# A two-layer recurrent kernel: the same instructions in another order on three engines

## Chip, cores and metric

The kernel runs on one core of one Trainium2 chip. The metric is device time in microseconds (us) of one execution, taken as the median of several executions. A smaller number is better.

## What is computed

The input `x` is 64 sequences (B) of 64 steps (S) of 256 features (D), all float32. Two layers are added to it one after the other.

```python
# layer 0: gated, written with cumulative sums (no step-by-step dependence in the matmuls)
f = sigmoid(x @ W_f.T + b_f); i = sigmoid(x @ W_i.T + b_i)
r = f / (f + i + EPS);        q = i / (f + i + EPS)
cand = x @ W_h.T + b_h
L = cumsum(log(r + EPS), axis=1)                  # over the 64 steps
scaling_t = exp(L_last - L_(t-1))                 # product of (r + EPS) from t to the end
hidden = cumsum(scaling * q * cand, axis=1) + exp(L) * cond
x1 = x + hidden
# layer 1: a plain recurrence of 64 dependent steps
h_t = tanh(x1_t @ Wx + b + h_(t-1) @ Wh),   h_0 = cond
out = x1 + h
```

## The kernel before

Features lie on the 128 partitions (two halves of 128), and the columns are steps times batch. The 64 steps are cut into eight chunks of eight steps, so a whole chunk of a tensor is 128 partitions by 1024 columns, and one step is 128 by 128. Each engine has its own instruction list, written out by hand as a list of calls; engines run their lists strictly in that order and meet through semaphores. There is no scheduler: what a list holds is what runs, and an instruction that waits holds up all that stand behind it on its engine.

**Layer 0, the gates.** The chunks are handled backwards, n = 0 being chunk 7, because the suffix product runs from the last step to the first.

- TensorE: `transpose_x(n)` turns a chunk of `x` (8 transposes, into one fixed pair of PSUM banks, free again when `chunk_split(n-1)` is done and filled from rows that a DMA has landed). `transpose_w(g)` turns weight g. `gates(n, g)` makes 12 matmuls of 512 columns for gate g (products of a high and a low part, so it needs `x_hi`, `wt_hi`, `wt_lo` and, for its last third, `x_lo`). `candidate(m)` does the same for the candidate, in the chunk order 7, 6, 5, 0, 3, 4, 1, 2. `transpose_cond` turns the initial state.
- ScalarE: `split_x(n)` and `split_w(g)` copy the rounded high part out of PSUM; `layer1_weight` does so for `Wx`. `sigmoids(n)` is four activations of 512 columns. `inverses((n, ...))` loads another table of functions, takes Ln and Exp of the denominators (1/den), and the next `sigmoids` loads the first table again. `move_candidate(c)` copies a candidate from PSUM to SBUF.
- VectorE: `chunk_split(n)` and `weight_split(g)` take the low part by subtraction. `denominator(n)` adds the gates; `ratio(n)` and `i_by_den(n)` multiply by the inverse. `suffix(n, t)`, 128 columns, multiplies the suffix product by one more step, t from 7 down to 0; each needs the one before it. `by_suffix` multiplies q by the suffix products, `product`, `product_first` and `moved_product` by the candidate.

**Between the layers.** `chain(c, s, e)` runs the cumulative sum and the cumulative product over steps s to e (instructions of 128 columns in two interleaved chains), `plus_decay` and `first_layer` add up `x1` in the tile `den`; chunks 0 and 1 do so in halves of four steps. For chunks 2 to 7 ScalarE's `split_x1` and VectorE's `x1_rest` split `x1` into high and low parts for TensorE.

**Layer 1.** TensorE adds `h @ Wh` to the projections `x1 @ Wx` in PSUM, ScalarE does the tanh, 64 steps one after the other. Projections of the next chunk and transposes of the output are put into the slots between the recurrence's matmuls, two slots to a step. The first steps use only the first half of chunk 0; TensorE waits for the second half of it in slot 6 and for all of chunk 1 in slot 9:

```python
for bank in SECOND_HALF.get(slot, ()):
    pe.wait_ge(x1_ready, 2)
    project_native(0, bank, second_half)
```

While VectorE finishes layer 0, TensorE runs matmuls whose results nobody reads (`keep_warm`), each released by a semaphore of VectorE's.

The line numbers of the profile that matter: L263 `split_x`, L267 `split_w`, L278 `sigmoids`, L286 and L289 `inverses`, L299 `layer1_weight`, L316 `split_x1`, L395 `chunk_split`, L400 `weight_split`, L409 `denominator`, L415 `ratio`, L419 `i_by_den`, L445 `suffix`, L541 and L537 `first_layer`, L546 `x1_rest`, L503 and L511 `chain`, L770 and L781 transposes, L790 to L796 gates and candidates, L903 and L911 projections, L932 the recurrence.

Of the kernel before, what the change touches and what calls it, by code (L numbers as in the profile page):

```python
# [26 lines left out]
def build(nc, x, cond, w_f, b_f, w_i, b_i, w_h, b_h, wx, wh, b_x, out):  # L27
# [10 lines left out]
    with ExitStack() as ctx:  # L38
# [107 lines left out]
        def chunk_of(n):  # L146
            return NCH - 1 - n
# [105 lines left out]
        def _(act):  # L253
# [7 lines left out]
            def split_x(n):  # L261
                act.wait_ge(xt_in_psum, n + 1)
                nc.scalar.activation(x_hi[:, chunk_of(n)], ps[:, XT:XT + 2], ACT.Copy).then_inc(x_hi_ready, 1)  # L263

            def split_w(g):
                act.wait_ge(wt_in_psum, g + 1)
                nc.scalar.activation(wt_hi[:, g], ps[:, WT[g]].rearrange("p (a h) -> p a h", a=HALVES), ACT.Copy)\  # L267
                    .then_inc(wt_hi_ready, 1)
# [28 lines left out]
            def layer1_weight():  # L297
                act.wait_ge(wx_landed, 16)
                nc.scalar.activation(wx_hi[:, :, :], wx_f[:, :, :], ACT.Copy).then_inc(wt_hi_ready, 1)  # L299
# [28 lines left out]
            def move_candidate(c):  # L328

                m = CAND_ORDER.index(c)  # L330
                if MOVED_TO[c] == "den 3":
                    act.wait_ge(i_inv_ready, NCH)
                    act.wait_ge(u_ready, NCH)
                if MOVED_TO[c] == "den 2":
                    act.wait_ge(i_inv_ready, NCH - 1)
                    act.wait_ge(u_ready, NCH - 1)
                if MOVED_TO[c] == "rows 0":
                    act.wait_ge(xt_in_psum, NCH - 1)
                if MOVED_TO[c] == "rows 1":
                    act.wait_ge(xt_in_psum, NCH)  # L340
                for a in range(HALVES):
                    act.wait_ge(cand_in_psum, 2 * m + a + 1)
                    nc.scalar.activation(MOVED[c][:, a], ps[:, CAND_BANK[m] + a], ACT.Identity,
                                         bias=bias[:, 2, a:a + 1]).then_inc(cand_moved, 1)

            split_x(0)
            split_w(0)
            split_w(1)
            split_w(2)
            split_x(1)  # L350
            sigmoids(0)
            split_x(2)
            inverses((0,))
            sigmoids(1)
            split_x(3)
            layer1_weight()
            first_state()
            sigmoids(2)
            split_x(4)
# [11 lines left out]
            inverses((7,))  # L371
            move_candidate(4)
            move_candidate(1)
            nc.scalar.preload_act_table_set("sigmoid_and_others")
            move_candidate(2)
            for c in range(NCH):
                for t in range(T):
                    tanh(c, t)
# [12 lines left out]
        def _(dve):  # L391
# [6 lines left out]
            def weight_split(g):  # L398
                dve.wait_ge(wt_hi_ready, g + 1)
                nc.vector.tensor_tensor(wt_lo[:, g], ps[:, WT[g]].rearrange("p (a h) -> p a h", a=HALVES),  # L400
                                        wt_hi[:, g].bitcast(F32), ALU.subtract).then_inc(wt_lo_ready, 1)
# [10 lines left out]
            def ratio(n):  # L412
                c = chunk_of(n)
                dve.wait_ge(inv_ready, n + 1)
                nc.vector.tensor_tensor(r_d[:, c + 1], r_d[:, c + 1], den[:, n % RING], ALU.mult).then_inc(u_ready, 1)  # L415

            def i_by_den(n):
                dve.wait_ge(inv_ready, n + 1)
                nc.vector.tensor_tensor(q_s[:, chunk_of(n)], q_s[:, chunk_of(n)], den[:, n % RING], ALU.mult)\  # L419
                    .then_inc(i_inv_ready, 1)  # L420
# [167 lines left out]
            chunk_split(1)  # L588
            denominator(0)
            chunk_split(2)  # L590
            i_by_den(0)
            ratio(0)
            weight_split(2)
            chunk_split(3)
            denominator(1)
            suffix(0, 7)
            suffix(0, 6)
            suffix(0, 5)
            suffix(0, 4)
            suffix(0, 3)  # L600
            denominator(2)
            chunk_split(4)
            suffix(0, 2)
            suffix(0, 1)
            suffix(0, 0)
            by_suffix(0)
            product(7)
            ratio(1)
            ratio(2)
            suffix(1, 7)  # L610
            suffix(1, 6)
            suffix(1, 5)
            suffix(1, 4)
            i_by_den(1)
            suffix(1, 3)
            suffix(1, 2)
            layer1_weight_rest()
            suffix(1, 1)
            chunk_split(5)
            suffix(1, 0)  # L620
            suffix(2, 7)
            suffix(2, 6)
            by_suffix(1)
            suffix(2, 5)
            suffix(2, 4)
            suffix(2, 3)
            suffix(2, 2)
            suffix(2, 1)
            denominator(3)
            denominator(4)  # L630
            chunk_split(6)
            i_by_den(2)
            suffix(2, 0)
            ratio(3)
            i_by_den(3)
            suffix(3, 7)
            suffix(3, 6)
            i_by_den(4)
            suffix(3, 5)
            suffix(3, 4)  # L640
            suffix(3, 3)
            chunk_split(7)
            suffix(3, 2)
            denominator(5)
            suffix(3, 1)
            ratio(4)
            suffix(3, 0)
            suffix(4, 7)
            by_suffix(2)
            suffix(4, 6)  # L650
            suffix(4, 5)
            denominator(6)
            suffix(4, 4)
            suffix(4, 3)
            suffix(4, 2)
            suffix(4, 1)
            product(6)
            suffix(4, 0)
            i_by_den(5)
            ratio(5)  # L660
            ratio(6)
            suffix(5, 7)
            denominator(7)
            suffix(5, 6)
            product(5)
            suffix(5, 5)
            suffix(5, 4)
            suffix(5, 3)
            suffix(5, 2)
            suffix(5, 1)  # L670
            suffix(5, 0)
            suffix(6, 7)
            suffix(6, 6)
            suffix(6, 5)
            suffix(6, 4)
            i_by_den(6)
            suffix(6, 3)
            suffix(6, 2)
            suffix(6, 1)
            ratio(7)  # L680
            suffix(6, 0)
            suffix(7, 7)
            suffix(7, 6)
            suffix(7, 5)
            suffix(7, 4)
            i_by_den(7)
            suffix(7, 3)
            suffix(7, 2)
            suffix(7, 1)
            suffix(7, 0)  # L690
            by_suffix_first(0)
            product_first(0)
            chain(0, 0, 4)
            plus_decay(0, 0)
            by_suffix_first(1)
            by_suffix(6)
            first_layer(0, 0)
            product_first(1)
            moved_product(1)
            chain(0, 4, 8)  # L700
            chain(1, 0, 4)
            plus_decay(0, 1)
            plus_decay(1, 0)
            first_layer(0, 1)
            chain(1, 4, 8)
            product(3)
            plus_decay(1, 1)
            first_layer(1, 0)
            first_layer(1, 1)
            by_suffix(5)  # L710
# [2 lines left out]
            chain(2, 4, 8)  # L713
            plus_decay(2, None)
            first_layer(2, None)
            by_suffix(4)
            by_suffix(3)
            x1_rest(2, 0)
            x1_rest(2, 1)
            moved_product(4)  # L720
            chain(3, 0, 4)
            chain(3, 4, 8)
            plus_decay(3, None)
            first_layer(3, None)
            x1_rest(3, 0)
            x1_rest(3, 1)
            chain(4, 0, 4)
            chain(4, 4, 8)
            plus_decay(4, None)
            first_layer(4, None)  # L730
            x1_rest(4, 0)
            chain(5, 0, 4)
            x1_rest(4, 1)
            chain(5, 4, 8)
            plus_decay(5, None)
            chain(6, 0, 4)
            chain(6, 4, 8)
            first_layer(5, None)
            chain(7, 0, 4)
            chain(7, 4, 8)  # L740
            x1_rest(5, 0)
            x1_rest(5, 1)
            plus_decay(6, None)
            first_layer(6, None)
            plus_decay(7, None)
            first_layer(7, None)
            x1_rest(6, 0)
            x1_rest(6, 1)
            x1_rest(7, 0)
            x1_rest(7, 1)  # L750
            out_sum_first()
# [10 lines left out]
        def _(pe):  # L762
# [98 lines left out]
            transpose_x(0)  # L861
            transpose_w(0)
            transpose_w(1)
            gates(0, 0)
            transpose_x(1)
            transpose_w(2)
            transpose_cond()
            gates(0, 1)
            transpose_x(2)
            gates(1, 0)  # L870
            gates(1, 1)
            transpose_x(3)
# [1 line left out]
            gates(2, 1)  # L874
            transpose_x(4)
            candidate(0)
            transpose_x(5)
            gates(3, 0)
            gates(3, 1)
            gates(4, 0)  # L880
            gates(4, 1)
# [4 lines left out]
            transpose_x(7)  # L886
            gates(6, 0)
            gates(6, 1)
            gates(7, 0)
            gates(7, 1)  # L890
            candidate(2)
            candidate(3)
            candidate(4)
            candidate(5)
# [160 lines left out]
```

## Time and profile before

| what | value |
|---|---|
| median of 3 executions | 194.7 us (194.15 to 194.71) |
| profiled execution, its own time | 194.83 us |
| its span in the trace | 193.0 us |
| busy over the span: TensorE, VectorE, ScalarE | 180.9, 131.7, 115.4 us |
| mean granted TensorE clock | 0.987 of full |

The span runs from the first instruction to the last; 1.8 us of the execution's time lie outside it. Busy time is a sum over stages that have different limits: VectorE does most of its work in the first 130 us, TensorE's busy time includes the matmuls that only keep it going.

### The profile page before, as it was taken

How to read it: one execution, taken by the hardware profiler on the slowest of the kernel's cores; microseconds unless marked ns; L12 is line 12 of the kernel's file. 1: busy time of each engine (PE TensorE's matmuls, PEld its weight loads, DVE VectorE, ACT ScalarE, POOL GpSimd, SP SyncE). 2: the span in 40 equal slices, each digit the busy share in tenths (PEclk: the TensorE clock that was granted, in tenths of full speed). 3: DMA queues.
4: the chain of work that ended last, by engine and by line, in shares of the span. 5: the costliest groups of instructions: out<-in, count | busy, mean ns of one | idle time of the engine just before them, and what ended most of it. 6: DMA issues, size and time to landing. Idle time of an engine off the chain costs nothing.

```text
span 193.0 us, 3133 instructions
## 1 busy us (share of the span) xinstructions
PE 180.9 (94%) x1178; PEld 161.4 (84%) x1178; DVE 131.7 (68%) x292; ACT 115.4 (60%) x235; POOL 24.4 (13%) x28
## 2 busy tenths in 40 slices
PE   6799999999999995999989999999999999999990
PEld 6678878888888884787879989999999999999880
DVE  0044569999998999999999999795999520200121
ACT  3309998996996897162223264656556565645550
POOL 1000000200100011131011210222211222221000
PEclk9999999999999998899999999999999999999998
DMA  5994340750320019299003035625374473627326
GB/s 112 246 250 115 109 109 19 171 138 3 59 51 0 0 33 184 41 190 192 15 5 54 5 49 93 128 41 131 51 153 69 77 141 56 135 38 154 59 48 169
DMA packets 12910, 17.83 MB, mean 92 GB/s; under 512 B 2080, under 2 KB 10720, under 8 KB 12896
## 3 DMA queue, kind: packets, MB, share of 16 engines
q0 software_dynamic: 4960, 7.87, 24.8%
q1 hardware_dynamic: 6848, 9.77, 19.5%
q10 hardware_dynamic: 1088, 0.00, 0.3%
q8 instruction: 9, 0.15, 0.3%
q14 instruction: 5, 0.04, 0.1%
HBM read 5.57 MB, written 4.19 MB: 51 GB/s over the span
## 4 chain that ended last, share of the span: by engine, by line
PE 53%; DVE 23%; ACT 14%; issue 5%; DMA 2%; SPq 0%; DVEq 0%
PE ps L932 29%; PE ps L903 9%; DVE suf L445 6%; DVE den L409 3%; PE ps L941 3%; PE ps L911 3%; ACT den L289 3%; DMA x_rows<-in_x 2%; PE ps L790 2%; ACT L278 2%; PE ps L796 2%; DVE q_s L430 2%; PE ps L792 2%; PE ps L781 2%; DVE q_s L419 2%
## 5 line engine op out<-in xcount | busy, mean ns | idle before, releaser
L932 PE MATMUL ps<-h_t,wh_f 128*128 128x128 f32 x504 | 69.3, 278 | 1.0 <-ACT h_t L309 0.7
L309 ACT ACTIVATE h_t<-ps,bias 128x64 f32<-128x64 f32 x128 | 37.2, 314 | 49.1 <-PE ps L932 43.7
L932 PEld LDWEIGHTS ps<-h_t,wh_f 128*128 128x128 f32 x504 | 62.2, 191 | 4.4 <-ACT h_t L309 3.3
L790 PE MATMUL ps<-x_hi,wt_lo 128*128 128x512 f32 x96 | 38.8, 404 | 3.1 <-DVE q_s L457 2.1
L792 PE MATMUL ps<-x_hi,wt_hi 128*128 128x512 f32 x96 | 38.2, 398 | 0.0
L796 PE MATMUL ps<-x_lo,wt_hi 128*128 128x512 f32 x96 | 30.3, 398 | 0.0
L243 POOL DMA_DIRECT2D den<-h_t x14 | 16.7, 1191 | 73.4 <-ACT h_t L309 73.4
L790 PEld LDWEIGHTS ps<-x_hi,wt_lo 128*128 128x128 f32 x96 | 18.3, 191 | 7.6 <-issue 3.9
L796 PEld LDWEIGHTS ps<-x_lo,wt_hi 128*128 128x128 f32 x96 | 18.5, 194 | 4.3 <-DVE x_lo L395 0.3
L792 PEld LDWEIGHTS ps<-x_hi,wt_hi 128*128 128x128 f32 x96 | 18.3, 191 | 3.6
L445 DVE SCALAR_TENSOR_TENSOR suf<-r_d,suf 128x128 f32<-128x128 f32 x64 | 18.5, 290 | 1.8
L546 DVE TENSOR_TENSOR x_lo<-den,x_hi 128x512 fp32r<-128x512 f32 x12 | 8.0, 692 | 16.6 <-ACT x_hi L316 16.6
L511 DVE SCALAR_TENSOR_TENSOR r_d<-r_d 128x128 f32<-128x128 f32 x64 | 18.6, 290 | 0.1
L503 DVE TENSOR_TENSOR q_s<-q_s 128x128 f32<-128x128 f32 x63 | 18.3, 291 | 0.0
L235 POOL DMA_DIRECT2D x_lo<-x_hi x8 | 7.0, 877 | 80.2 <-PE ps L796 80.2
L903 PE MATMUL ps<-x_hi,wx_lo 128*128 128x256 f32 x48 | 14.6, 319 | 0.0
L395 DVE TENSOR_TENSOR x_lo<-ps,x_hi 128x1024 fp32r<-128x1024 f32 x8 | 9.8, 1222 | 6.6 <-ACT x_hi L263 6.6
L903 PE MATMUL ps<-x_hi,wx_hi 128*128 128x256 f32 x48 | 13.6, 296 | 0.0
L278 ACT ACTIVATE q_s<-ps,bias 128x512 f32<-128x512 f32 x16 | 10.6, 692 | 3.4 <-PE ps L796 3.4
L263 ACT ACTIVATE x_hi<-ps 128x1024 fp32r<-128x1024 f32 x8 | 8.3, 1032 | 6.0 <-PE ps L781 6.0
L419 DVE TENSOR_TENSOR q_s<-q_s,den 128x1024 f32<-128x1024 f32 x8 | 9.8, 1220 | 2.2 <-ACT den L289 2.2
L409 DVE SCALAR_TENSOR_TENSOR den<-r_d,q_s 128x1024 f32<-128x1024 f32 x8 | 9.7, 1221 | 1.7 <-ACT q_s L278 1.6
(62 smaller groups left out, 232.3 us busy)
## 6 DMA issues: line engine op xcount, KB each, us to landing
x_rows<-in_x SPq DMA_DIRECT2D x16, 256.0 KB, 4.2
x_lo<-x_hi POOLq DMA_DIRECT2D x8, 512.0 KB, 5.2
den<-h_t POOLq DMA_DIRECT2D x14, 256.0 KB, 3.8
out_x<-x_rows SPq DMA_DIRECT2D x14, 256.0 KB, 3.2
out_x<-x_rows SPq DMA_DIRECT2D x2, 192.0 KB, 2.7
h_t<-in_L_cond_W_f SPq DMA_DIRECT2D x1, 256.0 KB, 4.8
h_t<-in_L_cond_W_i SPq DMA_DIRECT2D x1, 256.0 KB, 6.1
h_t<-in_L_cond_W_h SPq DMA_DIRECT2D x1, 256.0 KB, 7.4
```

Of the source, the lines that this page charges most:

```text
L243: nc.gpsimd.dma_start(den[:, c % RING, :, half_cols(th)], h_t[:, c % 2, :, half_cols(th)], accum_op=ALU.add).then_inc(o_sum[c % 2][th], 16)
L278: nc.scalar.activation(to, ps[:, 2 * g + a], ACT.Sigmoid, bias=bias[:, g, a:a + 1])\
L309: nc.scalar.activation(h_t[:, c % 2, a, cols(t)], ps[:, 4 * (c % 2) + 2 * a + t % 2, cols(t // 2)], ACT.Tanh, bias=bias[:, 3, a:a + 1])\
L409: nc.vector.scalar_tensor_tensor(den[:, n % RING], r_d[:, c + 1], EPS, q_s[:, c], ALU.add, ALU.add)\
L445: nc.vector.scalar_tensor_tensor(suf[:, n % SUF, :, cols(t)], r_d[:, c + 1, :, cols(t)], EPS, after, ALU.add, ALU.mult).then_inc(suf_steps, 1)
L503: nc.vector.tensor_tensor(now, now, before, ALU.add).then_inc(s_steps, 1)
L511: nc.vector.scalar_tensor_tensor(now, now, EPS, before, ALU.add, ALU.mult).then_inc(d_steps, 1)
L790: last = nc.tensor.matmul(to, w_lo[:, dk, rows], x_hi[:, c, dk], start=dk == 0, stop=False, skip_group_check=True)
L792: last = nc.tensor.matmul(to, w_hi[:, dk, rows], x_hi[:, c, dk], start=False, stop=False, skip_group_check=True)
L796: last = nc.tensor.matmul(to, w_hi[:, dk, rows], x_lo[:, c, dk], start=False, stop=dk == 1, skip_group_check=True)
L903: nc.tensor.matmul(ps[:, 4 * (c % 2) + bank, steps.start * B:steps.stop * B], w[:, part, a * P:(a + 1) * P], moving, start=first, stop=Fal ...
L932: return nc.tensor.matmul(bank[:, :, cols(t // 2)], wh_f[:, dk, a * P:(a + 1) * P], twice, start=False, stop=dk == 1, skip_group_check=True)
```

## The change

No instruction is added or taken out. Three lists are put into another order; every call keeps its waits and its semaphores.

```diff
@@ ScalarE @@
+            split_w(0)
             split_x(0)
-            split_w(0)
+            split_x(1)
             split_w(1)
             split_w(2)
-            split_x(1)
+            layer1_weight()
             sigmoids(0)
...
             split_x(3)
-            layer1_weight()
             first_state()
...
             move_candidate(1)
+            move_candidate(2)
             nc.scalar.preload_act_table_set("sigmoid_and_others")
-            move_candidate(2)
@@ VectorE, from denominator(0) to the suffix products of n = 1 @@
             denominator(0)
             chunk_split(2)
-            i_by_den(0)
             ratio(0)
+            suffix(0, 7)
             weight_split(2)
-            chunk_split(3)
-            denominator(1)
-            suffix(0, 7)
             suffix(0, 6)
             suffix(0, 5)
             suffix(0, 4)
             suffix(0, 3)
-            denominator(2)
-            chunk_split(4)
             suffix(0, 2)
             suffix(0, 1)
             suffix(0, 0)
+            chunk_split(3)
+            denominator(1)
+            i_by_den(0)
+            denominator(2)
+            layer1_weight_rest()
+            chunk_split(4)
             by_suffix(0)
             product(7)
...
```

From here to n = 7 the `denominator`, `i_by_den`, `ratio`, `chunk_split` and `product` calls are put between other `suffix` calls than before (one at a time rather than in groups of two to four; `product(6)` and `product(5)` come earlier). After the last suffix product:

```diff
             by_suffix_first(0)
             product_first(0)
+            by_suffix_first(1)
+            by_suffix(6)
             chain(0, 0, 4)
             plus_decay(0, 0)
-            by_suffix_first(1)
-            by_suffix(6)
+            product_first(1)
             first_layer(0, 0)
-            product_first(1)
             moved_product(1)
             chain(0, 4, 8)
+            plus_decay(0, 1)
             chain(1, 0, 4)
-            plus_decay(0, 1)
-            plus_decay(1, 0)
             first_layer(0, 1)
             chain(1, 4, 8)
+            plus_decay(1, 0)
+            plus_decay(1, 1)
             product(3)
-            plus_decay(1, 1)
             first_layer(1, 0)
             first_layer(1, 1)
...
             first_layer(2, None)
+            x1_rest(2, 0)
             by_suffix(4)
-            by_suffix(3)
-            x1_rest(2, 0)
             x1_rest(2, 1)
-            moved_product(4)
             chain(3, 0, 4)
             chain(3, 4, 8)
             plus_decay(3, None)
             first_layer(3, None)
+            by_suffix(3)
+            moved_product(4)
             x1_rest(3, 0)
             x1_rest(3, 1)
...
             first_layer(4, None)
+            chain(5, 0, 4)
+            chain(5, 4, 8)
             x1_rest(4, 0)
-            chain(5, 0, 4)
+            chain(6, 0, 4)
             x1_rest(4, 1)
-            chain(5, 4, 8)
@@ TensorE @@
             transpose_w(0)
             transpose_w(1)
+            transpose_x(1)
             gates(0, 0)
-            transpose_x(1)
             transpose_w(2)
-            transpose_cond()
             gates(0, 1)
             transpose_x(2)
+            transpose_cond()
             gates(1, 0)
...
             candidate(0)
+            gates(3, 0)
             transpose_x(5)
-            gates(3, 0)
             gates(3, 1)
...
             gates(6, 1)
+            candidate(2)
             gates(7, 0)
             gates(7, 1)
-            candidate(2)
             candidate(3)
```

## Rows read from the trace of the kernel before

**Rows 1.** Stretches of the span: length, busy time of each engine, granted clock, DMA.

```profile
28.00:99.00 71.00, 67.87 (x329) 56.20 (x327) 67.71 (x137) 49.74 (x65) 7.02 (x8) 0.98 0.38 76
99.00:188.00 89.00, 88.01 (x726) 84.40 (x726) 53.55 (x143) 48.53 (x149) 16.67 (x14) 1.00 0.44 80
```

**Rows 2.** Waits: who waited for whom, us in total, times, longest.

```profile
DVE x_lo L395 <- ACT x_hi L263: 6.6, 3, 4.5
DVE q_s L419 <- ACT den L289: 2.2, 1, 2.2
DVE den L409 <- ACT q_s L278: 1.6, 2, 1.2
...
PE ps L911 <- DVE den L541: 0.7, 1, 0.7
```

**Rows 3.** VectorE's timeline: start, us, instruction, idle before it and releaser.

```profile
9.23 0.69 DVE L400 TENSOR_TENSOR wt_lo<-ps,wt_hi 128x512 fp32r<-128x512 f32 x1 [8.20 <-ACT wt_hi L267]
...
27.84 1.23 DVE L395 TENSOR_TENSOR x_lo<-ps,x_hi 128x1024 fp32r<-128x1024 f32 x1 [1.68 <-ACT x_hi L263]
...
75.22 3.32 DVE L445 SCALAR_TENSOR_TENSOR suf<-r_d,suf 128x128 f32<-128x128 f32 x10
...
91.26 0.69 DVE L541 TENSOR_TENSOR den<-den,q_s 128x512 f32<-128x512 f32 x1
...
102.34 1.30 DVE L541 TENSOR_TENSOR den<-den,q_s 128x512 f32<-128x512 f32 x2
```

**Rows 4.** Chain of work that ended last, 96 to 100 us: start, us, what.

```profile
96.09 0.20 DVE q_s L503
...
98.96 0.71 PE ps L911 x4
```

**Rows 5.** ScalarE's timeline in the first 32 us.

```profile
7.69 1.02 ACT L263 ACTIVATE x_hi<-ps 128x1024 fp32r<-128x1024 f32 x1 [5.46 <-PE ps L781]
...
9.45 0.60 ACT L267 ACTIVATE wt_hi<-ps 128x512 fp32r<-128x512 f32 x1 [0.24 <-PE ps L770]
...
17.11 1.37 ACT L278 ACTIVATE q_s<-ps,bias 128x512 f32<-128x512 f32 x2
...
22.09 1.06 ACT L289 ACTIVATE den<-den 128x1024 f32<-128x1024 f32 x1
...
31.02 0.69 ACT L278 ACTIVATE q_s<-ps,bias 128x512 f32<-128x512 f32 x1 [0.67 <-PE ps L796]
```

**Rows 6.** TensorE's timeline in the first 18 us.

```profile
7.49 0.60 PE L770 MATMUL ps<-ident,h_t 128*128 128x128 f32 x4
8.75 0.66 PE L770 MATMUL ps<-ident,h_t 128*128 128x128 f32 x4 [0.66 <-DMA h_t<-in_L_cond_W_i]
...
14.73 0.50 PE L790 MATMUL ps<-x_hi,wt_lo 128*128 128x512 f32 x1
...
17.13 0.62 PE L796 MATMUL ps<-x_lo,wt_hi 128*128 128x512 f32 x2
17.59 1.03 PE L781 MATMUL ps<-ident,x_rows 128*128 128x128 f32 x8
```

**Rows 7.** The DMAs of the second chunk of x, issued at 3.14 and 3.66 us.

```profile
DMA to landing us min/median/max: 6.5/6.9/7.4
```

**Rows 8.** TensorE's timeline after its longest pause before the recurrence.

```profile
74.79 0.47 PE L790 MATMUL ps<-x_hi,wt_lo 128*128 128x512 f32 x1 [2.10 <-DVE q_s L457]
```

**Rows 9.** The stretch behind that pause (columns as Rows 1).

```profile
75.60:79.00 3.40, 3.40 (x10) 2.66 (x9) 3.03 (x10) 0.38 (x1) 0.00 (x0) 0.51 0.42 77
```

**Rows 10.** ScalarE's timeline in the recurrence: splits of x1.

```profile
112.93 1.14 ACT L316 ACTIVATE x_hi<-den 128x512 fp32r<-128x512 f32 x2
...
131.28 0.62 ACT L316 ACTIVATE x_hi<-den 128x512 fp32r<-128x512 f32 x1
```

**Rows 11.** TensorE's timeline in the recurrence: first readers of the low parts.

```profile
116.32 0.40 PE L903 MATMUL ps<-x_lo,wx_hi 128*128 128x256 f32 x2
...
125.55 0.28 PE L903 MATMUL ps<-x_lo,wx_hi 128*128 128x256 f32 x1
```

More of the change, by code:

```diff
@@ L610, in _ @@
             suffix(1, 7)
+            i_by_den(1)
             suffix(1, 6)
@@ L613, in _ @@
             suffix(1, 4)
-            i_by_den(1)
             suffix(1, 3)
             suffix(1, 2)
-            layer1_weight_rest()
             suffix(1, 1)
+            suffix(1, 0)
             chunk_split(5)
-            suffix(1, 0)
+            denominator(3)
             suffix(2, 7)
+            by_suffix(1)
             suffix(2, 6)
-            by_suffix(1)
+            i_by_den(2)
             suffix(2, 5)
+            denominator(4)
             suffix(2, 4)
             suffix(2, 3)
+            product(6)
             suffix(2, 2)
+            chunk_split(6)
             suffix(2, 1)
[L629 to L632, printed above, removed]
+            ratio(3)
             suffix(2, 0)
-            ratio(3)
+            suffix(3, 7)
+            by_suffix(2)
+            suffix(3, 6)
             i_by_den(3)
-            suffix(3, 7)
-            suffix(3, 6)
-            i_by_den(4)
             suffix(3, 5)
             suffix(3, 4)
+            i_by_den(4)
             suffix(3, 3)
-            chunk_split(7)
             suffix(3, 2)
-            denominator(5)
             suffix(3, 1)
@@ L648, in _ @@
             suffix(4, 7)
-            by_suffix(2)
+            chunk_split(7)
             suffix(4, 6)
+            denominator(5)
             suffix(4, 5)
@@ L655, in _ @@
             suffix(4, 2)
+            product(5)
             suffix(4, 1)
-            product(6)
+            ratio(5)
             suffix(4, 0)
+            suffix(5, 7)
+            suffix(5, 6)
             i_by_den(5)
[L660 to L665, printed above, removed]
             suffix(5, 5)
@@ L669, in _ @@
             suffix(5, 2)
+            ratio(6)
             suffix(5, 1)
@@ L672, in _ @@
             suffix(6, 7)
+            denominator(7)
             suffix(6, 6)
@@ L675, in _ @@
             suffix(6, 4)
-            i_by_den(6)
             suffix(6, 3)
@@ L679, in _ @@
             suffix(6, 1)
+            i_by_den(6)
             ratio(7)
@@ L683, in _ @@
             suffix(7, 6)
+            i_by_den(7)
             suffix(7, 5)
             suffix(7, 4)
-            i_by_den(7)
             suffix(7, 3)
@@ L730, in _ @@
             first_layer(4, None)
+            chain(5, 0, 4)
+            chain(5, 4, 8)
             x1_rest(4, 0)
-            chain(5, 0, 4)
+            chain(6, 0, 4)
             x1_rest(4, 1)
-            chain(5, 4, 8)
             plus_decay(5, None)
-            chain(6, 0, 4)
+            first_layer(5, None)
             chain(6, 4, 8)
-            first_layer(5, None)
             chain(7, 0, 4)
@@ L743, in _ @@
             plus_decay(6, None)
+            plus_decay(7, None)
             first_layer(6, None)
-            plus_decay(7, None)
-            first_layer(7, None)
             x1_rest(6, 0)
             x1_rest(6, 1)
+            first_layer(7, None)
             x1_rest(7, 0)
```

## Prediction

> **What bounds the kernel now.** I read the busy times by stretch first. From 28 to 99 us VectorE is busy 67.7 of 71.0 us, so layer 0 ends when VectorE has worked through its list; from 99 to 188 us TensorE is busy 88.0 of 89.0 us, so layer 1 takes the time of its matmuls [rows 1]. Between them stands one wait: TensorE waited 0.7 us for VectorE's `first_layer(0, 1)` and went on at 98.96 [rows 2, 4]. What the change can win is therefore how much earlier VectorE hands over `x1`, as far as the recurrence behind it then keeps its pace.
>
> The second view is VectorE's waits for ScalarE: 6.6 us in three waits of `chunk_split`, 2.2 us before the first use of an inverse, 1.6 us in two of `denominator`, 10.4 us in all [rows 2]. VectorE starts at 9.23 [rows 3]. Up to `first_layer(1, 1)`, which ends at 103.64 [rows 3], the old and the new list hold exactly the same instructions. So its new end follows from three differences: the start, the waits, and the bubbles between dependent instructions.
>
> **The start.** `transpose_w(0)` ends at 8.09 [rows 6]. With `split_w(0)` first, ScalarE runs it from 8.13 to 8.73 and `split_x(0)` from 8.65 to 9.67 (0.60 and 1.02 us, the next one starting 0.1 early) [rows 5]. VectorE's `weight_split(0)` starts at 8.77: 0.46 us won.
>
> **The waits, worked out one by one.** (1) `weight_split(0)` ends at 9.46, `chunk_split(0)` starts at 9.71: 0.25. (2) `transpose_x(1)` now stands ahead of `gates(0, 0)`. Its data were issued at 3.66 and take 7.4 us, so they land at 11.1 [rows 7]; the transposes end at 12.16 (1.03 us [rows 6]), `split_x(1)` at 13.23, `split_w(1)` at 13.75. `chunk_split(0)` ended at 10.93, `weight_split(1)` starts at 13.79: 2.86. (3) `gates(0, 0)` start at 11.95 and hold TensorE 2.86 us, as the pair from 14.73 to 17.59 does [rows 6]; `transpose_w(2)` takes some 0.5, and `gates(0, 1)` run from 15.3 to about 18.3, where before they ended at 17.75 (17.13 + 0.62) [rows 6]. I take them 0.5 us late, between 0.3, if the groups overlap more closely, and 0.7. The last of `sigmoids(0)` ended at 18.48 [rows 5] and now ends at 18.98. `chunk_split(1)` ended at 15.6: 3.4 for `denominator(0)`. ScalarE has `split_w(2)` and `layer1_weight` to do ahead of `sigmoids(0)`, but it waited for the gates anyway. (4) Everything that depends on `denominator(0)` is 0.5 late: the inverse ends at 23.65 instead of 23.15 [rows 5]. VectorE is free at 21.45: 2.25. (5) Here is the main gain. Before, VectorE then waited 1.68 us for `split_x(3)`, until 27.84 [rows 3]. Now `ratio(0)` and all eight `suffix(0, t)` with `weight_split(2)` stand there: from 23.7 they last until 28.1, and `chunk_split(3)` starts 0.5 late, at 28.34: 0.25. (6) `chunk_split(3)`, `denominator(1)` and `i_by_den(0)` last until 31.85; the last of `sigmoids(2)` ends 0.5 late, at 32.2 (31.02 + 0.69 + 0.5) [rows 5]: 0.4 for `denominator(2)`. After that I find none: each later sigmoid, split or inverse is ready before its turn on VectorE, the closest by 0.1 to 0.3 us, because VectorE is handed its work in smaller portions. The sum is 0.25 + 2.86 + 3.4 + 2.25 + 0.25 + 0.4 = 9.4 against 10.4: 1.0 us won.
>
> **The bubbles.** Ten suffix steps behind each other take 3.32 us, about 0.33 each [rows 3]; a 128-column step that has another instruction before it takes 0.20 [rows 4]. A suffix directly behind a suffix thus costs 0.12 more. The old list has 42 such pairs, the new one 39: 0.4 won. One more pair crosses a chunk, and `suffix(0, 7)` now stands right behind the `ratio` that it needs: 0.2 lost. Net 0.2. So the spreading of the suffix steps is, in spite of its many lines, the smallest term.
>
> **Sum and hand-over.** 0.46 + 1.0 + 0.2 = 1.7 us, with bounds of 1.5 and 2.0 from the 0.3 to 0.7 of step (3). `first_layer(0, 0)`, which lets the recurrence begin, gains less: `product_first(1)`, two instructions of 256 columns, now stands ahead of it. With 0.20 us for 128 columns [rows 4] and 0.61 for 512 (two in 1.30) [rows 3] that is about 0.8, and 0.2 of waiting is covered: 0.6 net. It ended at 91.95 [rows 3] and ends at 90.85. TensorE then needs 98.96 - 91.95 - 0.7 = 6.3 us to the place where it waits for `first_layer(0, 1)`: 97.15. That one gains 1.7 and another 0.6 by `plus_decay(1, 0)` being put behind it, 96.6, so the old wait is gone. Next TensorE needs `first_layer(1, 1)`: 103.64 - 1.7 = 101.94, about when TensorE arrives. Nothing new is late there, and the 1.7 us pass into the recurrence.
>
> **Cover behind the hand-over**, in times of before, since all shift together. `x1_rest(2, 0)` now follows `first_layer(2)` directly and waits for ScalarE's split, done at 113.55 [rows 10]; VectorE idles about 1.8 us. With `by_suffix(4)` (1.14) between, `x1_rest(2, 1)` ends at 116.0, and TensorE reads its result at 116.32 [rows 11]: 0.3 to spare. From 115.9: `chain(3)` 16 x 0.20, `plus_decay`, `first_layer` 2.5, `by_suffix(3)` and `moved_product(4)`, now behind them, 2.4, two `x1_rest` 1.3, gives 125.3 against the reader at 125.55 [rows 11]. `first_layer(4)` ends at 130.95, its split starts at 131.28 [rows 10]. So these cost nothing, but by 0.25 to 0.3 us only.
>
> **Edits at nothing.** `candidate(2)` ahead of `gates(7, g)` delays these by 2.86 us [rows 6], hidden by ScalarE, which is still at the inverses of 5 and 6; without that cover `denominator(7)` would be late by up to that much. `product(5)` earlier removes TensorE's pause of 2.10 us before 74.79 [rows 8]; TensorE only runs its idle matmuls the sooner. The table load behind `move_candidate(2)`, `transpose_cond` and `gates(3, 0)` move within free time of ScalarE and TensorE.
>
> **The likeliest case**: 194.83 - 1.7 = 193.1 on the profiled execution's scale; the median of the runs is 0.1 lower, so 193.0. Its own range is 192.4 to 193.4. Chance 0.46.
>
> **Rival 1: TensorE's clock falls at the start.** `transpose_w(1)` ends at 9.41 [rows 6] and TensorE now does nothing until 11.13, 1.7 us, behind an earlier pause of 0.66 [rows 6]. After the pause of 2.10 us before 74.79 the granted clock dropped: 0.51 over the 3.40 us from 75.6, the 1.2 GHz level [rows 8, 9]. In the early pauses of before it did not. The new pause lies between, so the row leaves this open. Such a stretch loses up to 0.49 x 3.40 = 1.67 us, here 1.3 to 1.67, and it falls on the gates that feed `sigmoids(0)`, with nothing to hide it. Of the 1.7 us some 0.2 stay: 194.4 (194.2 to 194.7). Chance 0.29. The Trainium skill ("TensorE: Matmul & The Clock Gate", Part 1) says that the clock follows how busy the engine has lately been and that this is judged in a rhythm that does not start with the kernel; by that rule some executions would give 193.0 and others 194.4, and no run shown here tells the share.
>
> **Rival 2: a cover is missed.** Step (6) found margins of 0.1 to 0.3 and the recurrence 0.25 to 0.3. If two or three are missed by 0.2 to 0.3 each, 0.3 to 1.0 is given back: 193.3 to 194.0, say 193.7. For it speaks that every margin is thin; against it that one miss costs only its own size. Chance 0.13.
>
> **Rival 3: slower, by the landing of x.** Before, `transpose_x(1)` came behind `gates(0, 0)`, so its data could land two us later than 11.1 and cost nothing. Now each microsecond of lateness is one on the path. From 12.8 on the gain is gone; past 13.4, with landings of over 9.7 us instead of 7.4 [rows 7], the kernel is slower, 195.4 and up. The trace has no landing that long on this queue. Chance 0.06.
>
> **The rest**, 0.06: the gates are hardly late and the waits (5) and (6) vanish as well, some 2.4 us, 192.4.
>
> **The numbers.** A measurement of this kernel can tell about 0.3% (0.6 us) from no change. Faster by that means under 194.1: 0.46 + 0.13 + 0.06 and a little of rival 1 = 0.67; within it, most of rival 1, 0.26; slower 0.07. The range from 192.3 to 194.6 leaves out rival 3, the ends of rival 1 and of the rest.
>
> **What would show it.** Right: `chunk_split(3)` starts near 28.3 with little idle time before it, `first_layer(1, 1)` ends near 101.9, TensorE's wait at `first_layer(0, 1)` is gone, and the recurrence keeps its pace. Rival 1: a granted clock near 0.5 somewhere between 10 and 16 us and `denominator(0)` past 20. Rival 2: new waits of VectorE for ScalarE between 33 and 85, or of TensorE or ScalarE for `x1_rest` or `first_layer` of chunks 2 to 4. Rival 3: `transpose_x(1)` starting after 12.8. I would be wrong outright if VectorE's end did not set the hand-over, or if the gates of n = 0 became much later than 0.7 us.

## The result, and the profile after

The changed kernel takes 194.09 us (median of 18 executions, 192.24 to 196.19) against 194.57 of the kernel before, run beside it (18, 194.11 to 195.14). Its executions fall in groups by the mean granted clock of TensorE: seven take 192.24 to 193.03 (clock 0.997 to 1.0), eight 193.91 to 194.70 (0.989 to 0.991). Three more, 195.92 to 196.19 at 0.975 or 0.976, lie beyond both and are left out of the ratio, which therefore is not that of the two medians: it is 0.9944, with a 95% interval of 0.9927 to 0.9962, faster by 0.56%. The medians of the two groups are 192.61 and 194.26, 1.65 us apart. So there are two results: one near what was forecast as the likeliest case (193.0), and one at what was forecast as Rival 1 (194.4).

The profiled execution (194.22, span 192.4) is of the second group. VectorE's timeline shows where it waited for ScalarE on the way to the hand-over (columns as [rows 3], which answer to these):

```profile
8.23 0.69 DVE L400 TENSOR_TENSOR wt_lo<-ps,wt_hi 128x512 fp32r<-128x512 f32 x1 [7.20 <-ACT wt_hi L267]
9.15 1.23 DVE L395 TENSOR_TENSOR x_lo<-ps,x_hi 128x1024 fp32r<-128x1024 f32 x1 [0.23 <-ACT x_hi L263]
14.03 0.69 DVE L400 TENSOR_TENSOR wt_lo<-ps,wt_hi 128x512 fp32r<-128x512 f32 x1 [3.66 <-ACT wt_hi L267]
20.39 1.23 DVE L409 SCALAR_TENSOR_TENSOR den<-r_d,q_s 128x1024 f32<-128x1024 f32 x1 [4.54 <-ACT q_s L278]
25.07 1.23 DVE L415 TENSOR_TENSOR r_d<-r_d,den 128x1024 f32<-128x1024 f32 x1 [2.24 <-ACT den L289]
...
29.72 1.22 DVE L395 TENSOR_TENSOR x_lo<-ps,x_hi 128x1024 fp32r<-128x1024 f32 x1 [0.34 <-ACT x_hi L263]
33.65 1.22 DVE L409 SCALAR_TENSOR_TENSOR den<-r_d,q_s 128x1024 f32<-128x1024 f32 x1 [0.43 <-ACT q_s L278]
...
91.48 0.68 DVE L541 TENSOR_TENSOR den<-den,q_s 128x512 f32<-128x512 f32 x1
97.06 0.68 DVE L541 TENSOR_TENSOR den<-den,q_s 128x512 f32<-128x512 f32 x1
101.80 1.28 DVE L541 TENSOR_TENSOR den<-den,q_s 128x512 f32<-128x512 f32 x2
```

The bracket at the end of a row is the idle time ahead of it. `denominator(0)` (L409) starts at 20.39, with 4.54 us of waiting where 3.4 was forecast, and `weight_split(1)` ahead of it waited 3.66 where 2.86 was; the six waits forecast one by one are all there, and no other until `first_layer(1, 1)` ends at 103.08. TensorE's timeline and two stretches of the span (columns as [rows 6] and [rows 1]) tell why these two are longer:

```profile
6.02 1.09 PE L781 MATMUL ps<-ident,x_rows 128*128 128x128 f32 x8 [0.70 <-DMA x_rows<-in_x]
6.95 0.61 PE L770 MATMUL ps<-ident,h_t 128*128 128x128 f32 x4
8.78 0.66 PE L770 MATMUL ps<-ident,h_t 128*128 128x128 f32 x4 [1.21 <-DMA h_t<-in_L_cond_W_i]
10.99 1.45 PE L781 MATMUL ps<-ident,x_rows 128*128 128x128 f32 x8 [1.56 <-DMA x_rows<-in_x]
...
12.67 0.63 PE L792 MATMUL ps<-x_hi,wt_hi 128*128 128x512 f32 x1
13.10 0.63 PE L790 MATMUL ps<-x_hi,wt_lo 128*128 128x512 f32 x1
...
15.36 0.39 PE L790 MATMUL ps<-x_hi,wt_lo 128*128 128x512 f32 x1
15.59 0.39 PE L792 MATMUL ps<-x_hi,wt_hi 128*128 128x512 f32 x1
```

```profile
11.60:15.00 3.40, 3.40 (x12) 2.83 (x11) 0.97 (x2) 1.51 (x2) 0.00 (x0) 0.50 1.07 275
15.00:18.40 3.40, 3.40 (x19) 2.80 (x18) 0.85 (x1) 1.49 (x3) 0.00 (x0) 1.00 0.37 88
```

TensorE stood still for 1.21 and then 1.56 us. From 11.60 to 15.00 its granted clock is 0.50, the 1.2 GHz level: the matmuls of `gates(0, 0)` follow each other by 0.43 us, while those behind 15.3 follow by 0.23. This is the stretch that Rival 1 named.

**One sum for all kernels.** In every profile of this study, before and after included, the span ends 89.31 to 89.41 us behind the end of `first_layer(1, 1)`. And that end is VectorE's start, plus its waits, plus the time of its instructions with the gaps between dependent ones. The remainder in the table is the end less start and waits:

| profile | VectorE starts | its waits | remainder | `first_layer(1, 1)` ends | us |
|---|---|---|---|---|---|
| before | 9.23 | 10.42 | 83.99 | 103.64 | 194.83 |
| after | 8.23 | 11.44 | 83.41 | 103.08 | 194.22 |
| e1_filled_pause | 8.43 | 9.39 | 83.40 | 101.22 | 192.36 |
| e2_start_of_before | 8.94 | 8.71 | 83.31 | 100.96 | 192.12 |
| e7_vector_old_filled | 8.70 | 11.32 | 84.07 | 104.09 | 195.25 |
| e9_first_part | 9.56 | 10.08 | 84.09 | 103.73 | 194.87 |
| e11_three_later | 8.68 | 8.91 | 84.09 | 101.68 | 192.84 |
| e6_vector_alone | 8.84 | 12.33 | 83.65 | 104.82 | 195.98 |
| e4_new_start | 8.42 | 8.42 | 83.39 | 100.23 | 191.37 |
| e10_waits_filled | 8.22 | 8.37 | 83.48 | 100.07 | 191.23 |
| e3_handover_filled | 8.45 | 9.36 | 83.41 | 101.22 | 192.40 |
| e5_pause_alone | 8.64 | 13.42 | 83.96 | 106.02 | 197.16 |
| e12_handover_old | 9.19 | 8.66 | 83.34 | 101.19 | 192.34 |
| e13_one_fill | 8.83 | 9.35 | 83.47 | 101.65 | 192.80 |

From before to after the start comes 1.00 earlier, the waits are 1.02 longer and the remainder is 0.58 shorter: 0.56 in all, and the execution is 0.61 shorter. Only 0.47 of the earlier start is the order: VectorE starts 1.14 us behind the end of `transpose_w(0)` before and 0.67 after. The rest is a difference between executions, in instructions that both lists have in the same place: the transposes of the first chunk, here in the kernel before, took 1.68 us against 1.09 in the rows above.

```profile
5.97 1.68 PE L781 MATMUL ps<-ident,x_rows 128*128 128x128 f32 x8 [0.25 <-DMA x_rows<-in_x]
```

### The profile page after: what moved, and what is told of

Its sections match the earlier page's. It is cut to its first block, busy times and chain, and to the rows that moved or that the text cites. A ratio compares the mean times of both kernels' runs of the same rounds, so it can differ in the third digit from the quotient of the medians.

```text
span 192.4 us, 3133 instructions
## 1 busy us (share of the span) xinstructions
PE 179.8 (93%) x1178; PEld 160.5 (83%) x1178; DVE 131.1 (68%) x292; ACT 115.4 (60%) x235; POOL 24.4 (13%) x28
## 3 DMA queue, kind: packets, MB, share of 16 engines
q0 software_dynamic: 4960, 7.87, 24.7%
## 4 chain that ended last, share of the span: by engine, by line
PE 48%; DVE 25%; issue 5%; ACT 2%; DVEq 0%
PE ps L932 31%; PE ps L903 9%; DVE suf L445 7%; PE ps L911 4%; DVE r_d L415 4%; DVE q_s L419 3%; PE ps L941 3%; DVE den L409 2%; DVE q_s L430 2%; DVE q_s L457 2%; ACT h_t L309 1%; DVE x_lo L395 1%; DVE q_s L484 1%; PE ps L950 1%; DVE q_s L466 1%
## 5 line engine op out<-in xcount | busy, mean ns | idle before, releaser
L511 DVE SCALAR_TENSOR_TENSOR r_d<-r_d 128x128 f32<-128x128 f32 x64 | 18.1, 282 | 0.1
L503 DVE TENSOR_TENSOR q_s<-q_s 128x128 f32<-128x128 f32 x63 | 17.8, 282 | 0.0
L409 DVE SCALAR_TENSOR_TENSOR den<-r_d,q_s 128x1024 f32<-128x1024 f32 x8 | 9.8, 1219 | 5.0 <-ACT q_s L278 5.0
L415 DVE TENSOR_TENSOR r_d<-r_d,den 128x1024 f32<-128x1024 f32 x8 | 9.7, 1218 | 2.2 <-ACT den L289 2.2
L278 ACT ACTIVATE r_d<-ps,bias 128x512 f32<-128x512 f32 x16 | 10.5, 698 | 0.7 <-PE ps L796 0.7
L781 PE MATMUL ps<-ident,x_rows 128*128 128x128 f32 x64 | 8.8, 282 | 2.3 <-DMA x_rows<-in_x 2.3
```

What stands on the lines that cost most here:

```text
L278: nc.scalar.activation(to, ps[:, 2 * g + a], ACT.Sigmoid, bias=bias[:, g, a:a + 1])\
L503: nc.vector.tensor_tensor(now, now, before, ALU.add).then_inc(s_steps, 1)
L511: nc.vector.scalar_tensor_tensor(now, now, EPS, before, ALU.add, ALU.mult).then_inc(d_steps, 1)
```

## The experiments

Ratios are to the kernel before, with their 95% intervals; the runs of before that went with each of the three sets had medians of 194.55 (e1 to e4), 194.50 (e5 to e9) and 194.74 (e10 to e13). Lines of `...` in a diff stand for lines left out.

### The clock at the start

**e1_filled_pause**: the changed kernel with idle matmuls (their product is not read) in both early pauses of TensorE.

```
             transpose_w(0)
+            fill(3)
             transpose_w(1)
+            fill(6)
             transpose_x(1)
```

> The changed kernel, with matmuls that nobody reads in TensorE's pause at the start: three behind transpose_w(0), six behind transpose_w(1). Theory A (the lower TensorE clock behind that pause is what splits the executions into some near 192.6, some near 194.2 and a few near 196): the group near 194.2 goes, nearly all executions lie between 192.2 and 193.1, median 192.7, granted clock 0.997 or more; a few with a second stretch of low clock at the hand-over may remain, near 194.4. Theory B (the landing of x varies, and the transposes that wait for it now stand on the path; the clock is only a sign of it): the spread stays as it is, 192.2 to 196.2, and the median stays near 194.

Measured: 192.70 (six executions, 192.30 to 192.96), ratio 0.9887 (0.9863 to 0.9911), clock 0.998 to 1.0 in all. The longer group is gone. TensorE's timeline and the stretch, of this kernel:

```profile
8.89 1.50 PE L776 MATMUL ps<-ident 128*128 128x128 f32 x12
10.72 1.06 PE L786 MATMUL ps<-ident,x_rows 128*128 128x128 f32 x8 [0.32 <-DMA x_rows<-in_x]
```

```profile
11.60:15.00 3.40, 3.40 (x19) 2.83 (x18) 1.64 (x2) 1.51 (x2) 0.00 (x0) 1.00 1.07 268
```

With the clock at 1.00 in the same stretch VectorE's six waits are 0.23, 2.79, 3.34, 2.24, 0.34 and 0.45. No work was taken away, some was added, and the kernel is faster: most of the loss is the clock's. (Of the 1.86 us by which `first_layer(1, 1)` ends earlier than in the profile above, 0.27 are an earlier start of `transpose_x(1)`, 10.72 against 10.99.)

**e13_one_fill**: only `fill(3)`, in the first pause.

> The changed kernel with three idle matmuls behind transpose_w(0), in the first of the two early pauses (1.2 us); the second, in which TensorE waits for the second chunk of x (1.6 us), stays. Theory A1 (the second pause alone is enough for the clock to fall in some executions): again two groups, 192.3 to 192.9 and 193.9 to 194.7, the long one with a granted clock 0.01 lower. Theory A2 (it takes both pauses): one group, 192.3 to 193.0, as with both filled.

Measured: 192.80 (four executions, 192.71 to 192.85), ratio 0.9902 (0.9886 to 0.9918). In this kernel's timeline the second pause is left, and is longer than it was:

```profile
11.11 1.06 PE L786 MATMUL ps<-ident,x_rows 128*128 128x128 f32 x8 [1.85 <-DVE x_lo L395]
```

None of the four is of the longer group. With unfilled pauses the shorter group holds 7 of the 18 executions above and 5 of the 8 of e3, so by chance that would happen some 5 times in 100 (12/26 to the fourth). It speaks for A2, that the last pause alone is not enough; four executions don't settle it. The profile of e3 (below), in which nothing is filled ahead of the hand-over, points the same way: it is of the shorter group, its first pause is 0.46 us and not 1.21, its second 1.84, and the clock stayed at 1.00.

```profile
8.24 0.66 PE L770 MATMUL ps<-ident,h_t 128*128 128x128 f32 x4 [0.46 <-DMA h_t<-in_L_cond_W_i]
10.73 1.06 PE L781 MATMUL ps<-ident,x_rows 128*128 128x128 f32 x8 [1.84 <-DVE x_lo L395]
...
11.60:15.00 3.40, 3.40 (x19) 2.83 (x18) 1.62 (x2) 1.51 (x2) 0.00 (x0) 1.00 1.08 275
```

**e5_pause_alone**: the kernel before, with the one move that makes the pause.

```
+            transpose_x(1)
             gates(0, 0)
-            transpose_x(1)
```

> The kernel before, with one edit: transpose_x(1) stands ahead of gates(0, 0) in TensorE's list. Theory A (the pause in which TensorE waits for the second chunk of x makes its clock fall in some executions, whatever stands around it): about half of the executions show a granted clock lower by 0.01 than the others, and are 1 to 2 us longer. Without the fall the gates of n = 0 come later by what the wait for x is long, with nothing to hide it: 195.2 to 195.6; with it 196.5 to 197.5; the median between. Theory B (the two groups of the changed kernel come from its new lists further on): one group, 195.2 to 195.6. Theory C (the pause and the later gates are hidden in this list): 194.5, like before.

Measured: 195.90, ratio 1.0074 (1.0049 to 1.0099). Four executions take 195.51 to 196.02, two 197.14 and 197.16. The profiled one is of the two, and its stretch shows the fall, now in the lists of before:

```profile
11.60:15.00 3.40, 3.40 (x12) 2.79 (x11) 0.00 (x0) 0.00 (x0) 0.00 (x0) 0.54 1.10 271
```

Theory A holds in size (1.4 us between the medians of the two groups), with two executions of six where it had about half. Without the fall the move costs 1.2 us, a little over what was expected.

**e3_handover_filled**: the changed kernel, the early pauses left, with other idle matmuls around the hand-over.

```
-                keep_warm(FILL, 2, COLS)
+                keep_warm(FILL, 7 if done is s_steps and count == 3 else 0 if done is x1_ready else 2, COLS)
```

> The changed kernel with the idle matmuls at the hand-over put elsewhere: seven instead of two behind the third prefix step, none behind first_layer(0, 0), where two stood in the recurrence's way. Theory A, second part (the executions near 196 have a further stretch of low clock behind TensorE's pause of 1.3 us before first_layer(0, 0)): the group near 196 goes, those near 192.6 and 194.2 stay in about equal shares; median about 193.5 to 194.2. If the low clock of the 196 group has another place, three of eighteen executions or so still lie near 196. The two matmuls taken off the path give at most 0.1 us, since TensorE then waits for first_layer(1, 1).

Measured: eight executions; five of 192.40 to 192.74, two of 194.10 and 194.41 (clock 0.989), one of 196.54 (0.993); ratio 0.9918 (0.9884 to 0.9953). Both groups are still there at the same times, so filling the hand-over does not remove the longer one. Where the executions near 196 lose their time stays open: no profile shows one. Up to the hand-over this is the changed kernel itself, and the profiled execution (192.40) is one of its shorter group: VectorE's waits in it are 0.22, 2.79, 3.33, 2.24, 0.35 and 0.43, as in e1, with no matmul added ahead of them.

### Which list carries the gain

**e2_start_of_before**: the changed kernel with the first entries of ScalarE's and TensorE's lists as before (`split_x(0)` first, `layer1_weight()` late, `gates(0, 0)` ahead of `transpose_x(1)`).

> The changed kernel, but the start of ScalarE's and TensorE's lists as before the change (gates(0, 0) ahead of transpose_x(1), split_x(0) first, layer1_weight late). Theory A: no long pause at the start, so no low clock there; VectorE keeps the win at chunk_split(3) and in the suffix steps. Counted step by step: denominator(0) back at 18.5, chunk_split(3) with 0.3 of waiting, 192.2 us, nearly all executions within 0.6 of each other. Theory B gives the same mean with a spread as of before. If the new start is a win of its own, as my sum had it (0.46 us from split_w(0) first against 0.5 lost with the gates), this kernel is within 0.5 us of the changed kernel's best executions.

Measured: 192.04 (six, 191.75 to 193.19), ratio 0.9866 (0.9836 to 0.9895). Without the new starts the median is 0.66 us below that with them and the pauses filled (0.4 by the ratios, whose intervals overlap), and 2.05 below the changed kernel's.

**e7_vector_old_filled**: the reverse, ScalarE's and TensorE's lists as changed with the pauses filled, and VectorE's whole list as before.

> The changed kernel with the early pauses filled as in the first experiment, and with VectorE's list of before. Theory V (VectorE's list carries the gain; the new starts of ScalarE and TensorE give nothing): 194.5 to 195.3, no gain over before. Theory S (the new starts carry it): about 192.7, as with VectorE's new list. By the prediction's own sum the start gives 0.46 us of it: 194.1. If the fill holds the clock up, no execution shows a granted clock lower by 0.01 or more than the rest.

Measured: 195.25 (nine, 194.62 to 195.56), ratio 1.0030 (1.0016 to 1.0044). These lists lose 0.6 to 0.75 us even with the clock at 1.00 from 11.60 to 15.00; Theory V holds. That no execution would show a lower clock was wrong: six of the nine have 0.986 to 0.989. The profiled one shows where, behind the pause of 2.10 us that VectorE's old list brings with it, as before [rows 8, 9]:

```profile
75.60:79.00 3.40, 3.40 (x10) 2.59 (x10) 2.99 (x12) 0.84 (x1) 0.00 (x0) 0.53 0.56 105
```

**e6_vector_alone**: the kernel before with VectorE's new list and nothing else.

> The kernel before with VectorE's new list alone; ScalarE's and TensorE's lists stay as before. Theory V (VectorE's new list carries the gain and needs nothing of the others): about 192.1, as the run with the start of before. Theory W (in VectorE's new list product(5) stands earlier, and needs candidate(2), which in TensorE's old list comes only behind gates(7, 0) and gates(7, 1)): VectorE waits some 2.5 to 3.5 us for TensorE near 69 us, nothing hides it, and all of the gain and more is gone: 195.2 to 196.2.

Measured: 196.08, ratio 1.0079 (1.0065 to 1.0094): slower. VectorE's timeline of it, at `product(5)` and at the end of the hand-over:

```profile
68.90 0.75 DVE L457 SCALAR_TENSOR_TENSOR q_s<-ps,bias,q_s 128x512 f32<-128x512 f32 x1 [2.88 <-PE ps L796]
70.15 0.75 DVE L457 SCALAR_TENSOR_TENSOR q_s<-ps,bias,q_s 128x512 f32<-128x512 f32 x1 [0.50 <-PE ps L796]
...
103.54 1.28 DVE L541 TENSOR_TENSOR den<-den,q_s 128x512 f32<-128x512 f32 x2
```

Theory W: `product(5)` comes earlier in the new list and needs `candidate(2)`, so TensorE's list has to follow. The move of `candidate(2)` spares VectorE's new list 3.4 us of waiting. No run has that move alone; in the kernel before no wait of VectorE for TensorE stands there that it could take away.

**e9_first_part**: as e2, with VectorE's list new only as far as `by_suffix(0)`, and as before from there on.

> The run with the start of before, in which VectorE's list is new only up to by_suffix(0) (ratio(0), the suffix steps of n = 0 and weight_split(2) ahead of chunk_split(3)), and that of before from there on. Theory P (as predicted: the gain is the wait of 1.68 us for split_x(3), and the spreading of the suffix steps gives 0.2): 192.2 to 192.6, nearly all of the 2.5 us. Theory Q (the rest of the list, which hands VectorE the work of later chunks in smaller portions and moves first_layer(0, 1) ahead of plus_decay(1, 0), gives the larger part): 193.6 to 194.2.

Measured: 194.17 (twelve, 194.02 to 194.89), ratio 0.9987 (0.9975 to 1.0000). Its VectorE timeline:

```profile
28.16 1.23 DVE L395 TENSOR_TENSOR x_lo<-ps,x_hi 128x1024 fp32r<-128x1024 f32 x1 [0.35 <-ACT x_hi L263]
32.08 1.22 DVE L409 SCALAR_TENSOR_TENSOR den<-r_d,q_s 128x1024 f32<-128x1024 f32 x1 [0.42 <-ACT q_s L278]
52.97 1.23 DVE L415 TENSOR_TENSOR r_d<-r_d,den 128x1024 f32<-128x1024 f32 x1 [0.26 <-ACT den L289]
58.57 1.23 DVE L395 TENSOR_TENSOR x_lo<-ps,x_hi 128x1024 fp32r<-128x1024 f32 x1 [0.72 <-ACT x_hi L263]
72.65 1.23 DVE L409 SCALAR_TENSOR_TENSOR den<-r_d,q_s 128x1024 f32<-128x1024 f32 x1 [0.46 <-ACT q_s L278]
```

The wait of 1.68 us for `split_x(3)` [rows 3] is down to 0.35, as predicted, and a wait of 0.42 for `denominator(2)` is new. Then VectorE, being early, meets ScalarE at `ratio(3)`, `chunk_split(7)` and `denominator(7)` and waits 1.44 us. From 27 us on its waits add up to 2.21, against 1.68 + 0.42 + 0.45 = 2.55 in the kernel before: the 1.3 us won at `split_x(3)` shrink to 0.34, which is what the runs show (194.50 - 194.17 = 0.33). Theory Q.

**e11_three_later**: as e9, with three instructions moved down the old part of the list.

```
-            chunk_split(7)
             suffix(3, 2)
-            denominator(5)
...
             suffix(4, 7)
+            chunk_split(7)
             by_suffix(2)
             suffix(4, 6)
+            denominator(5)
...
-            denominator(7)
...
             suffix(6, 7)
+            denominator(7)
```

> The run with only the first part of VectorE's new list, and three of its later instructions moved down the old list to about where the new one has them: chunk_split(7) and denominator(5) behind suffix(4, 7) and suffix(4, 6), denominator(7) behind suffix(6, 7). In the run without these moves VectorE waited 0.26, 0.72 and 0.46 us for ScalarE at ratio(3), chunk_split(7) and denominator(7). Theory Q1 (the first part's gain is lost in these waits, as VectorE there only reaches ScalarE's pace sooner): the last two vanish, 0.7 + 0.45 us are won: 192.7 to 193.2. Theory Q2 (the rest of the new list gains by fewer dependent pairs and by the order at the hand-over): no more than 0.3 won: 193.9 to 194.2.

Measured: 192.86 (four, 192.77 to 193.12), ratio 0.9908 (0.9891 to 0.9924). Behind `denominator(2)` one wait is left in its timeline:

```profile
52.13 1.23 DVE L415 TENSOR_TENSOR r_d<-r_d,den 128x1024 f32<-128x1024 f32 x1 [0.24 <-ACT den L289]
```

Theory Q1. Three instructions bring some 1.5 us (0.9987 to 0.9908 of 194.5), because they leave VectorE other work to do until ScalarE is ready: its waits are 1.17 us shorter than in e9 (8.91 against 10.08 in the table). The other 0.3 lies between two sets of runs and was not traced.

**e12_handover_old**: as e2, with VectorE's order of before from `by_suffix_first(0)` to `first_layer(1, 1)`.

> The run with the start of before, and VectorE's order of before between by_suffix_first(0) and first_layer(1, 1) (product_first(1) behind first_layer(0, 0), plus_decay(1, 0) ahead of first_layer(0, 1)). The prediction's step: first_layer(0, 0) comes 0.6 to 0.8 us earlier, first_layer(0, 1) 0.6 later, first_layer(1, 1) unchanged. If first_layer(1, 1) is what TensorE meets last (the prediction), the time stays at 192.0 to 192.3. If first_layer(0, 1) sets it, TensorE waits there again, as in the kernel before (0.7 us), and the time is 192.5 to 192.9.

Measured: 192.15 (four, 191.88 to 192.59), ratio 0.9871 (0.9851 to 0.9890), the same as e2. TensorE waits 0.6 us for `first_layer(0, 1)` again, and it costs nothing.

### Better starts

**e4_new_start**: the changed kernel with `gates(0, 0)` ahead of `transpose_x(1)` again, and `split_w(1)` ahead of `split_x(1)`; `split_w(0)` stays first.

> The changed kernel with a third order at the start: TensorE does gates(0, 0) ahead of transpose_x(1) as before, ScalarE does split_w(0), split_x(0), split_w(1), split_x(1), split_w(2) and sigmoids(0), layer1_weight late as before. Counted step by step: weight_split(0) 0.46 us earlier as in the changed kernel, denominator(0) 0.5 us earlier than before and 1.0 earlier than in the changed kernel, so 2.4 to 2.8 us less than before: 191.7 to 192.2. Theory A: no group near 194.2, since TensorE's pause at the start is short again. Theory B: no group near 194.2 either, since the landing of x is off the path; the two theories part at the filled pause.

Measured: 191.76 (six, 191.37 to 192.90), ratio 0.9848 (0.9818 to 0.9877). VectorE starts at 8.42, as in e1, and its first four waits are 0.23, 3.52, 1.63 and 2.24, or 7.62 together instead of 8.60. It beats before and after; from e2 (192.04) its executions don't set it apart.

**e10_waits_filled**: as e4, with more of VectorE's work put into those waits; ScalarE does `layer1_weight()` earlier for it, ahead of `split_x(1)`. VectorE's list against the changed kernel's:

```
             chunk_split(2)
+            weight_split(2)
+            layer1_weight_rest()
             ratio(0)
             suffix(0, 7)
-            weight_split(2)
...
             suffix(0, 0)
+            i_by_den(0)
             chunk_split(3)
             denominator(1)
-            i_by_den(0)
+            by_suffix(0)
             denominator(2)
-            layer1_weight_rest()
             chunk_split(4)
-            by_suffix(0)
```

> The run with the new start list, in which VectorE also does weight_split(2) and layer1_weight_rest() in the wait of 2.24 us ahead of ratio(0) (ScalarE copies the layer 1 weight earlier, in its own pause), and i_by_den(0) and by_suffix(0) ahead of where it waited for split_x(3) and denominator(2). Theory F (each wait of VectorE before the hand-over that is filled is won): the work of 0.6 + 0.6 us that moves into the wait, and the 0.34 and 0.46 us behind it, give 1.2 to 1.6 us: 190.3. Theory G (behind it VectorE only meets ScalarE's inverses of n = 1 and 2 sooner, whose time the table load and the gates set): a new wait of 1.5 to 2 us ahead of ratio(1), and 191.6 to 191.9 as without.

Measured: 191.60 (six, 191.23 to 192.87), ratio 0.9853 (0.9828 to 0.9879), as e4. Its VectorE timeline:

```profile
22.05 1.23 DVE L415 TENSOR_TENSOR r_d<-r_d,den 128x1024 f32<-128x1024 f32 x1 [1.04 <-ACT den L289]
30.62 1.23 DVE L409 SCALAR_TENSOR_TENSOR den<-r_d,q_s 128x1024 f32<-128x1024 f32 x1 [0.20 <-ACT q_s L278]
36.11 2.36 DVE L415 TENSOR_TENSOR r_d<-r_d,den 128x1024 f32<-128x1024 f32 x2 [1.73 <-ACT den L289]
```

Theory G: 1.80 us of waits are filled, and a new one of 1.73 stands ahead of `ratio(1)`, for the inverse.

## Why the prediction was right, and where not

- **The forecast.** 193.0 was the likeliest case: six of the seven executions of the shorter group lie within its own range of 192.4 to 193.4, the seventh at 192.24. The median of all, 194.09, is at the lower edge of the longer group, and it was luck on which side of the gap between the groups it fell; it lies in the forecast range because that range was made to hold both cases. In e1's profile `first_layer(1, 1)` ends at 101.22 where 101.94 was forecast: 0.34 by an earlier start of VectorE (8.43 against 8.77), 0.4 by the bubbles (below).
- **Rival 1 was given too little.** It had 0.29; 8 of the 18 executions are of its group and 3 lie beyond it, against 7 in the likeliest case (in e3, 2 and 1 of 8). Place and price were right: granted clock 0.50 between 11.6 and 15.0, 194.26 against 194.4. The Trainium skill ("TensorE: Matmul & The Clock Gate", Part 1) says that the clock follows the engine's recent activity, judged in a rhythm that does not start with the kernel. The executions agree in that one program gives two groups, 1.65 us apart. They don't show that the rhythm alone decides: the pauses differ between executions too, 1.21 and 1.56 us in the profile where the clock fell, 0.46 and 1.84 in that of e3, where it did not. Which of the two makes the groups was not tested.
- **The waits.** Forecast 0.25, 2.86, 3.4, 2.25, 0.25 and 0.4, measured in e1 0.23, 2.79, 3.34, 2.24, 0.34 and 0.45, and within 0.02 the same in e3: 9.4 against 9.39 and 9.36. No further one appeared, so Rival 2 fell. Rival 3 did too: `transpose_x(1)` starts at 10.99. Step (2) named the landing of x alone; in e3 and e13 the same pause ended with VectorE's `chunk_split(0)`, which frees the banks.
- **"Here is the main gain" was wrong as an account.** The wait at step (5) does shrink, but alone it is worth 0.3 us (e9). The sum was right only because its next sentence, that no later wait follows, holds for the whole new list; the kernel with the rest of the list (e2) is 2.5 us faster than before, and e11 shows that this sentence carries about half of that, 1.2 us by the waits and 1.5 by the time.
- **The bubbles were mis-sized.** 0.2 was forecast. The remainder in the table is 83.96 to 84.09 with the old spacing of the suffix steps and 83.31 to 83.48 with the new (83.65 in e6, with its waits for TensorE in between): 0.6. It comes from the steps of n = 1 to 7: e9, new for n = 0 alone, has 84.09, and e12, old at the hand-over alone, 83.34. The pairs counted in the prediction are right (42 and 39), so 0.12 us for each is too small a price or not the whole of it; which was not taken apart.
- **The start.** 0.46 was forecast, and counted from the end of `transpose_w(0)` 0.47 was measured; VectorE starts at 8.22 to 8.83 in seven profiles with `split_w(0)` first and at 8.64 to 9.56 in seven without, on average 0.5 earlier. But steps (1) to (4), all waits at the start, add up to 8.76 where before has 4.47 + 1.16 + 2.24 = 7.87. The sum thus held a loss of 0.4 for the new starts and did not say so; e7 against before has it at 0.6 to 0.75, e1 against e2 at 0.4 to 0.66.
- **Hand-over and cover.** Right: `first_layer(1, 1)` decides (e12), and the constant 89.3 to 89.4 behind it shows that the thin margins in the recurrence all held.
- **Edits at nothing.** `candidate(2)` costs nothing, but it is a condition of the new list (e6): the forecast had only its cost.

## What to carry to other kernels

Add up an engine's start, waits and work to the instruction that hands over, and a reordering can be costed in advance; but price the list as a whole, since a filled wait is only won if the next meeting with the same partner is moved too (e9, e11, e10). Where a reordering leaves TensorE idle ahead of work on the path, fill the pause with matmuls that nobody reads, or better, give it its next work first. And look at the single executions beside the median: here one program has two times.

## What was not expected of the hardware

Pauses of 1.21 and 1.56 us, with 0.66 us of matmuls between them, were enough for the granted clock to fall to 0.50 in the profiled execution, and 1.28 and 1.52 us for 0.54 in e5's. Pauses of 0.46 and 1.84 us (e3's profile) were not, nor was one of 1.85 us with the first filled (e13's). In the kernel before, executions with a mean clock of 0.986 to 0.988 take 194.30 to 195.12 in one set, those with 0.999 to 1.0 take 194.29 to 194.78: the medians are 0.4 us apart. Whether that is the fall behind 74.79 [rows 8, 9] or the start was not tested: in the profiles of before and of e9 the two come together, the fall and first transposes of 1.68 us instead of 1.09.
